# A fused three-stage decoder: new engine orders in the third stage, and a power instruction for twelve Newton operations

## The chip, the cores and the metric

One core of a Trainium2 chip runs the whole kernel. The metric is the device time of one execution in microseconds, as the median of several runs. Engines are named as the profile names them: PE (TensorE), DVE (VectorE), ACT (ScalarE), POOL (GpSimd), SP (SyncE, which here only issues transfers).

## The reference, cut to what matters

The input is 64 sequences of 64 tokens with 128 features. Three parts are added to x in turn: self attention with 16 heads of width 8, cross attention with 16 heads of width 64, and a stack of six layers of local attention and feed-forward. The change touches the third:

```python
for i in range(6):
    x = attn_layer(shift_tokens(x), Wqkv[i], q_scale[i], k_scale[i], Wo[i]) + x
    x = ffn_layer(shift_tokens(x), ln_g[i], ln_b[i], W1[i], b1[i], W2[i], b2[i]) + x

def attn_layer(x, Wqkv, qs, ksc, Wo):
    q, k, v = heads(x @ Wqkv)                    # 16 heads of 64
    q, k = l2norm(q) * qs, l2norm(k) * ksc       # t / max(norm(t), 1e-12)
    q, k = rotary(q), rotary(k)
    sim = q @ k.T * 8                            # causal, window of 32
    return (softmax(masked(sim)) @ v) @ Wo

def ffn_layer(x, g, bln, W1, b1, W2, b2):
    xn = (x - mean) / sqrt(var + 1e-5) * g + bln
    a, gate = split(xn @ W1 + b1)
    return a * gelu(gate) @ W2 + b2
```

`shift_tokens` moves the second half of the features down by one token. All arithmetic is in 32-bit floats.

## The kernel before

Two sequences make one tile of 128 tokens (partitions), so there are 32 tiles, and in the third stage 32 x 6 = 192 pairs of tile and layer, called tiles from here on. x stays in the on-chip buffers X and Y. The function `local` writes the third stage as five lists of instructions, one per engine, each a loop over i from 0 to 200. In round i an engine calls small functions, each for a tile that lies some rounds back: `query_rotary(i, 0)`, `probs_turned(i - 3, 1)`, `ff_added(i - 8)`. The work is thus a pipeline over nine tiles. The order of the calls in a round is written out by hand, and each engine works strictly in that order; semaphores count finished instructions. `Counted` turns "this half of this tile" into a count, given the order in which the halves come.

One tile goes through these steps (line numbers are those of the profile):

- SP copies Y, shifted, into `ystat` (three transfers, L1026 to L1028). PE turns it (`input_turned`), ACT copies it to `xcT`, and PE multiplies by the weights of queries (L1123), keys (L1153) and values (L1175).
- ACT squares queries (L1294) and keys (L1300). DVE rotates them: `query_rotary` (L1389) and `key_rotary` (L1403) each write two products for half of the heads, and POOL's accumulating transfers (`queries_added` L1520, `keys_added` L1526) add the two.
- The norms: query squares are summed by PE (`query_lengths`), key squares by DVE (`squares_summed`, L1424). `query_floor` (L1410) and `seeded` (L1431 to L1435) put both into `ssm`, 128 x 32, and make an integer first guess of 1/sqrt. POOL's `inverse_lengths` (L1567 to L1574) refines it with three Newton steps of four operations into `rn`.
- POOL scales keys by `rn` (`keys_scaled`, L1534), PE turns them (`keys_turned`), ACT copies them to `kT`, and PE computes `scores` (L1189, L1194). DVE takes the maximum (L1444) and subtracts it (L1450), POOL scales by the query lengths (`scores_scaled`, L1540), ACT takes exponents (L1317), DVE sums rows (L1465) and inverts (L1471), POOL normalises (`probs_scaled`, L1546).
- DVE turns the probabilities in blocks into Z (`probs_turned`, L1459); SP's `probs_moved` (L1048, L1049) moves blocks of Z between partitions with four transfers. PE multiplies by the values (`head_outputs`, L1224) and by Wo (`out_projection`, L1235), DVE adds the result to Y (`attention_added`, L1370).
- SP copies Y, shifted, into `ys` (`ff_input`, again L1026 to L1028). DVE takes `statistics` (L1417, L1419), POOL makes the deviation (`inverse_deviation`, L1552 to L1556, the middle one a power on 128 x 1), ACT applies it (`normalised`, L1327), PE turns it (`normal_turned`), ACT copies it with scale (`normal_out`, L1283). PE's `ff_in` (L1209), ACT's `gates` (L1334), DVE's `gated` (L1478), PE's `ff_out` (L1110) and DVE's `ff_added` (L1376) end the tile.

All eight PSUM banks are shared. `scores` uses bank 0, which `query_lengths` uses too, and bank 7, which first holds the keys of half 0; `ff_in` uses banks 2, 1 and 3, and bank 3 is also the one that `ff_added` reads. So `ff_in(t)` waits for `ff_added(t - 1)`, and `scores(t)` for the rotations of the next tile's keys. SP's order in a round is `layer_input(i + 1)` (`ystat`), `ff_input(i - 5)` (`ys`), then weights, if any, then `probs_moved(i - 3)`:

```python
def probs_moved(t):
    sp.wait_ge(s.p_turned.sem, s.p_turned.upto(0, t + 1))
    ...
layer_input(0)
for i in range(N + LAST + 1):
    layer_input(i + 1)
    ff_input(i - 5)
    ...
    probs_moved(i - 3)
```

Of the kernel before, what the change touches and what calls it, by code (L numbers as in the profile page):

```python
# [971 lines left out]
def local(nc, sem, m):  # L972
# [16 lines left out]
    s.x_turned, s.x_copied = sem("local_x_turned"), sem("local_x_copied")  # L989
    s.qk, s.squared, s.rotated = counted("qk", *four), counted("squared", (QUERIES, 0), (QUERIES, 1), (KEYS, 1), (KEYS, 0)), counted("rotated", *four)  # L990
    s.summed, s.seed, s.lengths = sem("local_summed"), sem("local_seed"), sem("local_lengths")
    s.q_lengths, s.q_lengths_copied = sem("local_q_lengths"), sem("local_q_lengths_copied")
# [4 lines left out]
    s.v, s.v_copied = counted("v", 1, 0), counted("v_copied", 1, 0)  # L997
    s.scores, s.mx, s.less = sem("local_scores"), counted("mx", 0, 1), counted("less", 0, 1)
    s.scaled, s.probs, s.row_sum = counted("scaled", 0, 1), counted("probs", 1, 0), counted("row_sum", 0, 1)
    s.inverse, s.normal = counted("inverse", 1, 0), counted("normal", 1, 0)  # L1000
# [89 lines left out]
    def _(pe):  # L1090
# [52 lines left out]
        def keys(t, half):  # L1143
            if exists(t):
                if half == 0:
                    pe.wait_ge(m.w_in, 64 * layer(t) + 64)
                    if t == 0:
                        pe.wait_ge(m.cross_y1, TILES)
                    at_least(pe, s.less.sem, s.less.upto(1, t - 1))
                if t < 2:  # L1150
                    at_least(pe, s.rotated.sem, s.rotated.upto((KEYS, half), t))
                cols = m.WA[:, layer(t) % 2, INNER:2 * INNER].rearrange("p (h z d) -> p z h d", z=2, d=32)
                mm(b[QK_BANK[KEYS, half]][:, :], m.xsT[:, t % 2, :], cols[:, half, :, :], start=True, stop=True)\  # L1153
                    .then_inc(s.qk.sem, 1)

        def keys_turned(t, j):
            if exists(t):
                pe.wait_ge(s.k_scaled.sem, s.k_scaled.upto(j, t + 1))
                if j == 1 and t == N - 1:
                    pe.wait_ge(s.y1, t - 3)  # L1160
                for n in range(4):
# [103 lines left out]
    def _(act):  # L1265
# [73 lines left out]
        for i in range(N + LAST + 1):  # L1339
# [15 lines left out]
            outputs_out(i - 4, 0)  # L1355
            values_out(i, 0)
            exponents(i - 2, 0)
# [5 lines left out]
    def _(dve):  # L1363
# [29 lines left out]
        def key_rotary(t, half):  # L1393

            if exists(t):
                dve.wait_ge(s.squared.sem, s.squared.upto((KEYS, half), t + 1))
                if half == 0:
                    at_least(dve, s.k_turned.sem, s.k_turned.upto(0, t))
# [27 lines left out]

        def seeded(t):
            if exists(t):
                ssm, bits = m.ssm[:, t % 2, :], m.bits[:, t % 2, :]
                dve.wait_ge(s.summed, t + 1)  # L1430
                nc.vector.tensor_scalar(ssm[:, 16:32], m.ss[:, t % 2, :], 1e-24, None, ALU.max).then_inc(s.seed, 1)  # L1431
                dve.wait_ge(s.seed, 3 * t + 1)
                nc.vector.tensor_scalar(bits, ssm.bitcast(I32), 1, None, ALU.arith_shift_right).then_inc(s.seed, 1)
                dve.wait_ge(s.seed, 3 * t + 2)
                nc.vector.tensor_scalar(m.seed[:, t % 2, :], bits, -1.0, RSQRT_MAGIC, ALU.mult, ALU.add)\  # L1435
                    .then_inc(s.seed, 1)

# [69 lines left out]
    def _(pool):  # L1507
# [15 lines left out]
        def keys_added(t):  # L1523
            if exists(t):
                pool.wait_ge(s.rotated.sem, s.rotated.upto((KEYS, 1), t + 1))
                pool.dma_start(m.RK[:, 0, :], m.RK[:, 1, :], accum_op=ALU.add).then_inc(s.k_added, 16)  # L1526

        def keys_scaled(t, j):
            if exists(t):
                if j == 1:  # L1530
                    pool.wait_ge(s.k_added, 16 * t + 16)
                    pool.wait_ge(s.lengths, 12 * t + 12)
                part = by_head(m.RK[:, 0, j * 512:(j + 1) * 512])
# [25 lines left out]
        def inverse_lengths(t):  # L1559
            if exists(t):  # L1560
                pool.wait_ge(s.seed, 3 * t + 3)
                y = m.seed[:, t % 2, :].bitcast(FP32)
                for step in range(3):
                    done = 12 * t + 4 * step
                    if step:
                        pool.wait_ge(s.lengths, done)
                    tt(m.rn_a[:, :], y, y, ALU.mult).then_inc(s.lengths, 1)  # L1567
                    pool.wait_ge(s.lengths, done + 1)
                    tt(m.rn_b[:, :], m.rn_a[:, :], m.ssm[:, t % 2, :], ALU.mult).then_inc(s.lengths, 1)
                    pool.wait_ge(s.lengths, done + 2)  # L1570
                    nc.gpsimd.tensor_scalar(m.rn_a[:, :], m.rn_b[:, :], -0.5, 1.5, ALU.mult, ALU.add)\
                        .then_inc(s.lengths, 1)
                    pool.wait_ge(s.lengths, done + 3)
                    tt(m.rn[:, t % 4, :], y, m.rn_a[:, :], ALU.mult).then_inc(s.lengths, 1)  # L1574
                    y = m.rn[:, t % 4, :]

        for i in range(N + LAST + 1):
            queries_added(i)
            probs_scaled(i - 3, 1)
            probs_scaled(i - 3, 0)  # L1580
            keys_added(i)
            inverse_deviation(i - 5)
            inverse_lengths(i)
# [54 lines left out]
```

## Time and profile before

| | us |
|---|---|
| median of 3 runs | 3696.78 (3694.6 to 3710.01) |
| profiled execution | 3706.61 |
| its span | 3704.8 |
| PE busy | 3253.5 (88%) |
| DVE busy | 2801.0 (76%) |
| POOL busy | 2652.6 (72%) |
| ACT busy | 2487.4 (67%) |

The span is that of one execution recorded by the hardware profiler, and the shares are of that span; the execution's own time lies 1.8 us over it and 9.8 us over the median of the runs. The third stage begins at about 560 us. An engine counts as busy while an instruction runs on it; issuing a transfer is not counted for SP.

### The profile page before, as it was taken

The numbers are of one execution on the slowest core, as the hardware profiler recorded it, in microseconds if no ns is written. First come the engines' busy times: TensorE is split into PE (matmuls) and PEld (weight loads), VectorE is DVE, ScalarE is ACT, GpSimd is POOL, SyncE is SP. The second block draws the span as 40 slices with busy tenths as digits, with TensorE's granted clock in tenths as the row PEclk, the third lists the DMA queues.
The fourth block names the chain that finished last, engine by engine and source line by source line (L and its number), as shares of the span: only waits on it lengthen the run. The fifth ranks groups of instructions, "written<-read, shape, count | busy, mean of one in ns | idle before, by whom it ended". The sixth has DMA issues, their size and how long they took to land.

```text
span 3704.8 us, 124977 instructions
## 1 busy us (share of the span) xinstructions
PE 3253.5 (88%) x51333; PEld 2530.0 (68%) x51333; DVE 2801.0 (76%) x5681; ACT 2487.4 (67%) x4952; POOL 2652.6 (72%) x5005
## 2 busy tenths in 40 slices
PE   8999997888888888888888888888888888888886
PEld 6778775666666666666666666766666666666665
DVE  6844446888787888887888878788778878888885
ACT  5756664676666767666667667677666766667664
POOL 5522227877787887787778877777777778777774
PEclk9999999999999999999999999999999999999999
DMA  4000004444445444444444444444444444444442
GB/s 96 3 8 8 8 6 96 102 95 94 87 103 109 92 93 90 100 104 97 94 93 89 101 104 97 90 93 95 103 103 94 95 88 98 94 98 90 97 95 52
DMA packets 280546, 310.50 MB, mean 84 GB/s; under 512 B 154281, under 2 KB 225582, under 8 KB 279982
## 3 DMA queue, kind: packets, MB, share of 16 engines
q0 software_dynamic: 58368, 201.36, 28.0%
q1 hardware_dynamic: 220892, 100.93, 10.7%
q8 instruction: 412, 6.75, 0.8%
q14 instruction: 152, 1.25, 0.1%
q10 hardware_dynamic: 722, 0.21, 0.0%
HBM read 23.63 MB, written 2.10 MB: 7 GB/s over the span
## 4 chain that ended last, share of the span: by engine, by line
PE 59%; DVE 25%; issue 8%; ACT 5%; POOL 1%; SPq 1%; DMA 1%; DVEq 0%; POOLq 0%
PE bank L1153 10%; PE bank L1235 8%; PE bank L1209 8%; PE bank L1123 8%; DVE RK L1403 6%; DVE Z L1459 6%; PE bank L1094 6%; DVE ss L1424 6%; PE bank L1110 4%; PE bank L1134 3%; ACT sq L1300 3%; ACT xnT L1283 2%; PE bank L709 2%; PE bank L722 2%; PE bank L731 2%
## 5 line engine op out<-in xcount | busy, mean ns | idle before, releaser
L1403 DVE TENSOR_TENSOR RK<-bank,tables 128x1024 f32<-128x1024 f32 x384 | 468.7, 1222 | 329.3 <-ACT sq L1300 326.2
L1209 PE MATMUL bank<-xnT,W 128*128 128x128 f32 (+1 forms) x2304 | 322.8, 294 | 350.0 <-DVE Y L1376 349.3
L1389 DVE TENSOR_TENSOR RQ<-bank,q_tables 128x1024 f32<-128x1024 f32 x384 | 452.1, 1219 | 153.3 <-ACT sq L1294 153.2
L1209 PEld LDWEIGHTS bank<-xnT,W 128*128 128x128 f32 (+1 forms) x2304 | 282.6, 190 | 371.0 <-issue 371.0
L1546 POOL TENSOR_TENSOR P<-P,inv_sum 128x512 f32<-128x512 f32 x384 | 505.7, 1634 | 5.7 <-DVE inv_sum L1471 5.7
L1534 POOL TENSOR_TENSOR RK<-RK,rn 128x512 f32<-128x512 f32 x384 | 400.2, 1042 | 28.4 <-POOL rn L1574 0.9
L1520 POOL DMA_DIRECT2D RQ<-RQ x384 | 350.1, 1041 | 97.2 <-DVE RQ L1389 90.2
L1153 PE MATMUL bank<-WA,xcT 128*128 128x512 f32 x768 | 376.8, 613 | 37.0 <-DVE P L1450 16.7
L1540 POOL TENSOR_TENSOR P<-P,rn 128x512 f32<-128x512 f32 x384 | 402.4, 1048 | 3.8 <-DVE P L1450 3.8
L1267 ACT ACTIVATE kT<-bank 128x512 f32<-128x512 f32 x384 | 229.5, 598 | 249.8 <-PE bank L1094 249.8
L1235 PE MATMUL bank<-WO,OT 128*128 128x128 f32 x3072 | 382.3, 278 | 0.0
L1175 PE MATMUL bank<-WV,xcT 128*128 128x512 f32 x768 | 380.5, 618 | 0.0
L1123 PE MATMUL bank<-xcT,WQ 128*128 128x128 f32 x3072 | 375.1, 275 | 2.4 <-ACT xcT L1267 2.2
L1235 PEld LDWEIGHTS bank<-WO,OT 128*128 128x128 f32 x3072 | 367.7, 196 | 0.0
L1123 PEld LDWEIGHTS bank<-xcT,WQ 128*128 128x128 f32 x3072 | 358.4, 192 | 4.3 <-ACT xcT L1267 4.3
L1267 ACT ACTIVATE V<-bank 128x512 f32<-128x512 f32 x384 | 231.4, 603 | 138.5 <-PE bank L1175 138.5
L1526 POOL DMA_DIRECT2D RK<-RK x192 | 168.3, 876 | 178.3 <-DVE RK L1403 168.3
L1094 PEld LDWEIGHTS bank<-ident,RK 128*128 128x128 f32 x1536 | 186.4, 141 | 111.6 <-issue 99.2
L1444 DVE TENSOR_REDUCE mx<-bank 128x8 f32<-128x512 f32 x384 | 262.0, 682 | 0.0
L1450 DVE TENSOR_TENSOR P<-bank,mx 128x512 f32<-128x512 f32 x384 | 260.6, 679 | 0.1
L1465 DVE TENSOR_REDUCE row_sum<-P 128x8 f32<-128x512 f32 x384 | 259.4, 676 | 0.0
L1459 DVE STREAM_TRANSPOSE Z<-P 128x512 f32<-128x512 f32 x384 | 248.7, 685 | 2.3 <-POOL P L1546 2.3
(166 smaller groups left out, 7567.4 us busy)
## 6 DMA issues: line engine op xcount, KB each, us to landing
RQ<-RQ POOLq DMA_DIRECT2D x384, 256.0 KB, 4.0
RK<-RK POOLq DMA_DIRECT2D x192, 512.0 KB, 4.7
Z<-Z SPq DMA_DIRECT2D x768, 64.0 KB, 2.5
WA<-in_wqkv SPq DMA_DIRECT2D x24, 256.0 KB, 2.8
ystat<-Y SPq DMA_DIRECT2D x192, 32.0 KB
ystat<-Y SPq DMA_DIRECT2D x384, 15.8 KB
ys<-Y SPq DMA_DIRECT2D x192, 32.0 KB
ys<-Y SPq DMA_DIRECT2D x384, 15.8 KB
```

What stands on the lines that cost most here:

```text
L1094: return nc.tensor.transpose(dst, src, m.ident[:, :])
L1123: last = mm(b[QK_BANK[QUERIES, j]][:, n * 128:(n + 1) * 128], m.WQ[:, layer(t) % 2, at:at + 128], m.xsT[:, t % 2, :], start=True, stop=True)
L1153: mm(b[QK_BANK[KEYS, half]][:, :], m.xsT[:, t % 2, :], cols[:, half, :, :], start=True, stop=True)\
L1209: last = mm(FF_BANK[c][0:rows, side * 128:(side + 1) * 128], m.W1[:, off + at:off + at + rows], m.xnT[:, t % 2, :], start=True, stop=True)
L1235: last = mm(OUT[:, 0:128], m.OT[:, t % 2, c * 128:c * 128 + 128], wo[:, c * 128:(c + 1) * 128], start=(c == 0), stop=(c == PAIRS - 1))
L1267: return nc.scalar.activation(dst, src, ACT.Copy)
L1389: tt(both, src.unsqueeze(1).to_broadcast([128, 2, 8, SEQ]), m.q_tables[:, layer(t), :, :].unsqueeze(2).to_broadcast([128, 2, 8, SEQ]), ALU ...
L1403: tt(both, src.unsqueeze(1).to_broadcast([128, 2, 16, 32]), tab.unsqueeze(2).to_broadcast([128, 2, 16, 32]), ALU.mult).then_inc(s.rotated. ...
L1459: nc.vector.transpose(m.Z[:, t % 2, a, 1:3, :].rearrange("p k (h n) -> p k h n", n=32), blocks)\
L1534: tt(part, part, wide(m.rn[:, t % 4, 16 + 8 * j:24 + 8 * j]), ALU.mult).then_inc(s.k_scaled.sem, 1)
L1540: tt(part, part, wide(m.rn[:, t % 4, a:16:2]), ALU.mult).then_inc(s.scaled.sem, 1)
L1546: tt(part, part, wide(m.inv_sum[:, t % 2, 8 * a:8 * a + 8]), ALU.mult).then_inc(s.normal.sem, 1)
```

## The change

On DVE `ff_added` moves from behind the transposes to right behind `statistics`, the keys are rotated half 1 first, the two transposes are parted, with the key floor and both maxima between them, and `seeded` keeps only its floor (`key_floor`). On ACT `keys_out(i - 1, 1)` moves behind the squares of keys, `normal_out` behind the second `keys_out`, and exponents, values and outputs are interleaved in another way. On POOL `queries_added` moves from the front to behind both scalings of probabilities, and `inverse_deviation` and `keys_added` come between these. `inverse_lengths` becomes one `pow` on 128 x 32. PE's order is the same, with two waits added. Cut to its core:

```diff
-    s.qk, ..., s.rotated = ..., counted("rotated", *four)
-    s.summed, s.seed, s.lengths = sem("local_summed"), sem("local_seed"), sem("local_lengths")
+    s.qk, ..., s.rotated = ..., counted("rotated", (QUERIES, 0), (QUERIES, 1), (KEYS, 1), (KEYS, 0))
+    s.summed, s.k_floor, s.lengths = sem("local_summed"), sem("local_k_floor"), sem("local_lengths")
...
         def keys(t, half):
                     at_least(pe, s.less.sem, s.less.upto(1, t - 1))
+                else:
+                    at_least(pe, s.h, 3 * (t - 7))
...
         def keys_turned(t, j):
-                if j == 1 and t == N - 1:
-                    pe.wait_ge(s.y1, t - 3)
+                if j == 1:
+                    at_least(pe, s.y1, t - 3)
...
     # ACT, one round
             squares(i, QUERIES, 1)
-            keys_out(i - 1, 1)
             squares(i, KEYS, 1)
+            keys_out(i - 1, 1)
             query_lengths_out(i)
-            normal_out(i - 6)
             squares(i, KEYS, 0)
             keys_out(i - 1, 0)
+            normal_out(i - 6)
+            exponents(i - 2, 1)
             values_out(i, 1)
-            exponents(i - 2, 1)
             outputs_out(i - 4, 1)
+            values_out(i, 0)
             outputs_out(i - 4, 0)
-            values_out(i, 0)
             exponents(i - 2, 0)
...
-        def seeded(t):
+        def key_floor(t):
             if exists(t):
                 dve.wait_ge(s.summed, t + 1)
...
         def less_maximum(t, a):
                 dve.wait_ge(s.mx.sem, s.mx.upto(a, t + 1))
+                at_least(dve, s.p_turned.sem, s.p_turned.upto(a, t - 1))
...
     # DVE, one round
             statistics(i - 5)
+            ff_added(i - 8)
+            key_rotary(i, 1)
+            query_floor(i)
             key_rotary(i, 0)
-            query_floor(i)
-            key_rotary(i, 1)
             squares_summed(i)
             probs_turned(i - 3, 1)
+            key_floor(i)
+            maximum(i - 1, 0)
+            maximum(i - 1, 1)
             probs_turned(i - 3, 0)
-            ff_added(i - 8)
-            seeded(i)
-            maximum(i - 1, 0)
-            row_sums(i - 2, 0)
+            less_maximum(i - 1, 1)
             less_maximum(i - 1, 0)
             row_sums(i - 2, 1)
-            maximum(i - 1, 1)
             attention_added(i - 4)
+            row_sums(i - 2, 0)
+            gated(i - 7)
             inverse_sums(i - 2, 1)
-            gated(i - 7)
-            less_maximum(i - 1, 1)
             inverse_sums(i - 2, 0)
...
         def keys_added(t):
-                pool.wait_ge(s.rotated.sem, s.rotated.upto((KEYS, 1), t + 1))
+                pool.wait_ge(s.rotated.sem, s.rotated.upto((KEYS, 0), t + 1))
...
         def inverse_lengths(t):
-                pool.wait_ge(s.seed, 3 * t + 3)
-                y = m.seed[:, t % 2, :].bitcast(FP32)
-                for step in range(3):
-                    done = 12 * t + 4 * step
-                    if step:
-                        pool.wait_ge(s.lengths, done)
-                    tt(m.rn_a[:, :], y, y, ALU.mult).then_inc(s.lengths, 1)
...
+                pool.wait_ge(s.k_floor, t + 1)
+                pool.wait_ge(s.q_floor, t + 1)
+                tt(m.rn[:, t % 4, :], m.ssm[:, t % 2, :], m.minus_half[:, :].to_broadcast([128, 32]), ALU.pow)\
+                    .then_inc(s.lengths, 1)
...
     # POOL, one round
-            queries_added(i)
             probs_scaled(i - 3, 1)
-            probs_scaled(i - 3, 0)
-            keys_added(i)
             inverse_deviation(i - 5)
+            keys_added(i)
+            probs_scaled(i - 3, 0)
+            queries_added(i)
             inverse_lengths(i)
```

DVE's queue in the steady part of the third stage, from the statistics to the first maxima, in the kernel before (L1376 is `ff_added`, L1459 the transposes, L1431 to L1435 `seeded`):

```order
L1417 BN_STATS stats<-ys 128x6
L1419 BN_AGGR mv<-stats 128x2
L1403 TENSOR_TENSOR RK<-bank,tables 128x2x512
L1410 TENSOR_SCALAR ssm<-bank 128x16
L1403 TENSOR_TENSOR RK<-bank,tables 128x2x512
L1424 TENSOR_REDUCE ss<-sq 128x16
L1459 STREAM_TRANSPOSE Z<-P 128x512 x2
L1376 TENSOR_TENSOR Y<-Y,bank 128x128
L1431 TENSOR_SCALAR ssm<-ss 128x16
L1433 TENSOR_SCALAR bits<-ssm 128x32
L1435 TENSOR_SCALAR seed<-bits 128x32
L1444 TENSOR_REDUCE mx<-bank 128x8
```

The same place in the changed kernel, whose lines from here on stand two or three off (L1378 is `ff_added`, L1457 the transposes):

```order
L1419 BN_STATS stats<-ys 128x6
L1421 BN_AGGR mv<-stats 128x2
L1378 TENSOR_TENSOR Y<-Y,bank 128x128
L1405 TENSOR_TENSOR RK<-bank,tables 128x2x512
L1412 TENSOR_SCALAR ssm<-bank 128x16
L1405 TENSOR_TENSOR RK<-bank,tables 128x2x512
L1426 TENSOR_REDUCE ss<-sq 128x16
L1457 STREAM_TRANSPOSE Z<-P 128x512
L1432 TENSOR_SCALAR ssm<-ss 128x16
L1441 TENSOR_REDUCE mx<-bank 128x8 x2
L1457 STREAM_TRANSPOSE Z<-P 128x512
L1448 TENSOR_TENSOR P<-bank,mx 128x512 x2
```

The feed-forward's addition now stands before the rotations, and the second transpose, for which SP's Z transfers wait, behind both maxima.

POOL's queue before, from the query transfers on (L1520 and L1526 are the accumulating transfers of queries and keys, L1546 scales probabilities, L1552 to L1556 make the deviation, L1567 to L1574 the first of three Newton steps):

```order
L1520 DMA RQ<-RQ 64x1024 x2
L1546 TENSOR_TENSOR P<-P,inv_sum 128x512 x2
L1526 DMA RK<-RK 128x1024
L1552 TENSOR_SCALAR vare<-mv 128x1
L1554 TENSOR_TENSOR rstd<-vare,minus_half 128x1
L1556 TENSOR_SCALAR nmr<-mv,rstd 128x1
L1567 TENSOR_TENSOR rn_a<-seed 128x32
L1569 TENSOR_TENSOR rn_b<-rn_a,ssm 128x32
L1571 TENSOR_SCALAR rn_a<-rn_b 128x32
L1574 TENSOR_TENSOR rn<-seed,rn_a 128x32
```

And in the changed kernel (L1544 scales probabilities, L1524 and L1518 are the transfers of keys and queries, L1561 the power, L1532 and L1538 the scalings of keys and scores):

```order
L1544 TENSOR_TENSOR P<-P,inv_sum 128x512
L1550 TENSOR_SCALAR vare<-mv 128x1
L1552 TENSOR_TENSOR rstd<-vare,minus_half 128x1
L1554 TENSOR_SCALAR nmr<-mv,rstd 128x1
L1524 DMA RK<-RK 128x1024
L1544 TENSOR_TENSOR P<-P,inv_sum 128x512
L1518 DMA RQ<-RQ 64x1024 x2
L1561 TENSOR_TENSOR rn<-ssm,minus_half 128x32
L1532 TENSOR_TENSOR RK<-RK,rn 128x512
L1538 TENSOR_TENSOR P<-P,rn 128x512
L1532 TENSOR_TENSOR RK<-RK,rn 128x512
L1538 TENSOR_TENSOR P<-P,rn 128x512
```

The query transfers now come after the keys' and the second scaling, and one instruction stands in the place of twelve.

## Rows read from the trace of the kernel before

**Rows 1.** L1417, the statistics: how often, ns min/median/max, first and last start.
```profile
L1417 DVE BATCH_NORM_STATS2 stats<-ys x192: 283/284/297, 632.8 to 3688.3; 128x6 f32<-128x128 f32 x192
```
**Rows 2.** Busy us by engine in one steady stretch; then PEclk, DMA share, GB/s.
```profile
2400.00:2800.00 400.00, 350.71 (x5401) 271.05 (x5401) 321.33 (x646) 278.39 (x549) 315.30 (x588) 0.99 0.46 97
```
**Rows 3.** Waits from 1200 to 3600 us: waiting <- releaser: us, times, longest.
```profile
PE bank L1209 <- DVE Y L1376: 273.8, 149, 2.2
...
DVE stats L1417 <- DMA ys<-Y: 32.6, 46, 3.8
```
**Rows 4.** PE's timeline, end of a tile: start, us, instruction, [idle before <-releaser].
```profile
2425.52 0.41 PE L1189 MATMUL bank<-causalb,identb 64*64 64x512 bf16 x4
2425.76 1.10 PE L1194 MATMUL bank<-kT,RQ 64*64 64x64 f32 x64
2428.70 1.57 PE L1209 MATMUL bank<-xnT,W 128*128 128x128 f32 x12 [1.83 <-DVE Y L1376]
```
**Rows 5.** SP's timeline in a quiet tile: first Z and last `ys`.
```profile
2150.06 0.69 SPq L1048 DMA_DIRECT2D Z<-Z  x1
...
2156.47 0.70 SPq L1028 DMA_DIRECT2D ys<-Y  x1
```
**Rows 6.** Transposes, last `ys` issue, statistics: first and last of 170 tiles (DVE, SP).
```profile
730.67 1.30 DVE L1459 STREAM_TRANSPOSE Z<-P 128x512 f32<-128x512 f32 x2
739.08 0.70 SPq L1028 DMA_DIRECT2D ys<-Y  x1
...
3458.64 1.29 DVE L1459 STREAM_TRANSPOSE Z<-P 128x512 f32<-128x512 f32 x2
3467.17 0.70 SPq L1028 DMA_DIRECT2D ys<-Y  x1
3469.02 0.29 DVE L1417 BATCH_NORM_STATS2 stats<-ys 128x6 f32<-128x128 f32 x1 [0.21 <-DMA ys<-Y]
```
**Rows 7.** DVE's timeline: two maxima steps, and statistics to key floor.
```profile
2413.00 0.68 DVE L1444 TENSOR_REDUCE mx<-bank 128x8 f32<-128x512 f32 x1
2413.60 0.68 DVE L1465 TENSOR_REDUCE row_sum<-P 128x8 f32<-128x512 f32 x1
...
2421.20 0.28 DVE L1417 BATCH_NORM_STATS2 stats<-ys 128x6 f32<-128x128 f32 x1
2423.60 1.22 DVE L1403 TENSOR_TENSOR RK<-bank,tables 128x1024 f32<-128x1024 f32 x1 [1.90 <-ACT sq L1300]
2424.83 1.22 DVE L1403 TENSOR_TENSOR RK<-bank,tables 128x1024 f32<-128x1024 f32 x1
2425.96 1.21 DVE L1424 TENSOR_REDUCE ss<-sq 128x16 f32<-128x1024 f32 x1
2427.08 1.29 DVE L1459 STREAM_TRANSPOSE Z<-P 128x512 f32<-128x512 f32 x2
2428.30 0.25 DVE L1376 TENSOR_TENSOR Y<-Y,bank 128x128 f32<-128x128 f32 x1
2428.47 0.16 DVE L1431 TENSOR_SCALAR ssm<-ss 128x16 f32<-128x16 f32 x1
```
**Rows 8.** Busy us by engine in 1 us while Z is issued; DMA share.
```profile
2428.00:2429.00 1.00, 0.30 (x3) 0.33 (x4) 0.93 (x6) 0.43 (x2) 0.43 (x2) 1.00 1.02 188
```
**Rows 9.** POOL's timeline: first Newton operation, keys scaled, and what it waits for.
```profile
2413.17 0.24 POOL L1567 TENSOR_TENSOR rn_a<-seed 128x32 f32<-128x32 f32 x1 [0.60 <-DVE seed L1435]
2417.09 1.04 POOL L1534 TENSOR_TENSOR RK<-RK,rn 128x512 f32<-128x512 f32 x1
2421.59 1.83 POOL L1520 DMA_DIRECT2D RQ<-RQ  x2 [0.44 <-DVE RQ L1389]
2426.34 0.87 POOL L1526 DMA_DIRECT2D RK<-RK  x1 [0.85 <-DVE RK L1403]
```
**Rows 10.** POOL's groups by form: power and addition on 128x1: busy us, mean ns.
```profile
L1554 POOL TENSOR_TENSOR rstd<-vare,minus_half 128x1 f32<-128x1 f32 x192 | 109.5, 570 | 16.0
...
L1552 POOL TENSOR_SCALAR vare<-mv 128x1 f32<-128x1 f32 x192 | 43.2, 225 | 34.7 <-DVE mv L1419 19.0
```

More of the change, by code:

```diff
@@ L989, in local @@
     s.x_turned, s.x_copied = sem("local_x_turned"), sem("local_x_copied")
-    s.qk, s.squared, s.rotated = counted("qk", *four), counted("squared", (QUERIES, 0), (QUERIES, 1), (KEYS, 1), (KEYS, 0)), counted("rotated", *four)
-    s.summed, s.seed, s.lengths = sem("local_summed"), sem("local_seed"), sem("local_lengths")
+    s.qk, s.squared, s.rotated = counted("qk", *four), counted("squared", (QUERIES, 0), (QUERIES, 1), (KEYS, 1), (KEYS, 0)), counted("rotated", (QUERIES, 0), (QUERIES, 1), (KEYS, 1), (KEYS, 0))
+    s.summed, s.k_floor, s.lengths = sem("local_summed"), sem("local_k_floor"), sem("local_lengths")
     s.q_lengths, s.q_lengths_copied = sem("local_q_lengths"), sem("local_q_lengths_copied")
@@ L997, in local @@
     s.v, s.v_copied = counted("v", 1, 0), counted("v_copied", 1, 0)
-    s.scores, s.mx, s.less = sem("local_scores"), counted("mx", 0, 1), counted("less", 0, 1)
-    s.scaled, s.probs, s.row_sum = counted("scaled", 0, 1), counted("probs", 1, 0), counted("row_sum", 0, 1)
+    s.scores, s.mx, s.less = sem("local_scores"), counted("mx", 0, 1), counted("less", 1, 0)
+    s.scaled, s.probs, s.row_sum = counted("scaled", 0, 1), counted("probs", 1, 0), counted("row_sum", 1, 0)
     s.inverse, s.normal = counted("inverse", 1, 0), counted("normal", 1, 0)
@@ L1396, in key_rotary @@
                 dve.wait_ge(s.squared.sem, s.squared.upto((KEYS, half), t + 1))
-                if half == 0:
+                if half == 1:
                     at_least(dve, s.k_turned.sem, s.k_turned.upto(0, t))
@@ L1425, in squares_summed @@
                                         ALU.add).then_inc(s.summed, 1)
-        def seeded(t):
+        def key_floor(t):
             if exists(t):
-                ssm, bits = m.ssm[:, t % 2, :], m.bits[:, t % 2, :]
                 dve.wait_ge(s.summed, t + 1)
[L1431 to L1436, printed above, removed]
+                nc.vector.tensor_scalar(m.ssm[:, t % 2, 16:32], m.ss[:, t % 2, :], 1e-24, None, ALU.max)\
+                    .then_inc(s.k_floor, 1)
         def by_head(ap):
@@ L1531, in keys_scaled @@
                     pool.wait_ge(s.k_added, 16 * t + 16)
-                    pool.wait_ge(s.lengths, 12 * t + 12)
+                    pool.wait_ge(s.lengths, t + 1)
                 part = by_head(m.RK[:, 0, j * 512:(j + 1) * 512])
@@ L1560, in inverse_lengths @@
             if exists(t):
-                pool.wait_ge(s.seed, 3 * t + 3)
-                y = m.seed[:, t % 2, :].bitcast(FP32)
-                for step in range(3):
-                    done = 12 * t + 4 * step
-                    if step:
-                        pool.wait_ge(s.lengths, done)
-                    tt(m.rn_a[:, :], y, y, ALU.mult).then_inc(s.lengths, 1)
[L1568 to L1575, printed above, removed]
+                pool.wait_ge(s.k_floor, t + 1)
+                pool.wait_ge(s.q_floor, t + 1)
+                tt(m.rn[:, t % 4, :], m.ssm[:, t % 2, :], m.minus_half[:, :].to_broadcast([128, 32]), ALU.pow)\
+                    .then_inc(s.lengths, 1)
         for i in range(N + LAST + 1):
+            probs_scaled(i - 3, 1)
+            inverse_deviation(i - 5)
+            keys_added(i)
+            probs_scaled(i - 3, 0)
             queries_added(i)
-            probs_scaled(i - 3, 1)
-            probs_scaled(i - 3, 0)
-            keys_added(i)
-            inverse_deviation(i - 5)
             inverse_lengths(i)
```

## The prediction

> **What bounds the kernel now.** I read the stage first, then the waits, then one tile on each engine. The third stage handles 192 tiles; the statistics instruction that each tile has once starts at 632.8 us for the first and at 3688.3 us for the last [rows 1], so one tile takes (3688.3 - 632.8) / 191 = 16.00 us. Times 191, that is nearly the whole kernel, and every number below is one of microseconds per tile. In a steady stretch of 400 us, 25 tiles, PE is busy 350.7 us, 14.0 per tile, DVE 12.9, POOL 12.6, ACT 11.1, with the clock at 0.99 of the 2.4 GHz level [rows 2]. PE is the fullest engine and yet idles: its one large wait stands before the feed-forward matmuls, 1.83 to 1.84 us per tile, released by DVE's addition at L1376 [rows 3, 4]. In a tile's timeline the scores end at 2426.86 and the feed-forward starts at 2428.70 [rows 4]; everything else on PE is back to back, so PE alone would need 16.00 - 1.83 = 14.17 per tile.
>
> Beside that stands a second circle, which the waits show only faintly: DVE waited 32.6 us for the `ys` transfers in this stretch, 46 times [rows 3]. It runs like this. When the second transpose into Z is done (L1459), SP issues four Z transfers, then three for `ystat`, then three for `ys`, strictly in that order. DVE's statistics at L1417 wait for the three `ys` to land, and the next tile's transposes stand behind the statistics on DVE. So every tile goes once through DVE and once through SP's queue. In a quiet tile SP starts the first Z at 2150.06 and the last `ys` at 2156.47 [rows 5], 6.4 us after the end of the transpose. Over the 170 tiles between 731 and 3470 us I find 6.92 us on average; the first has 739.08 - 731.97 = 7.11, the last 3467.17 - 3459.93 = 7.24 [rows 6]. From the last issue to the start of the waiting statistics are 3469.02 - 3467.17 = 1.85 us [rows 6] (the median of all that waited is 1.89). SP's half is 6.92 + 1.89 = 8.81. DVE's half, statistics at 2421.20 to the end of the transposes at 2428.37, is 7.17 [rows 7]. Together 15.98 of a period of 16.00: this circle is almost as tight as PE's.
>
> **The change part by part.**
> *DVE's addition `ff_added` moves up,* from behind both transposes to right behind the statistics. PE's feed-forward then no longer waits for it: worth up to 1.83, if nothing else is late. What is late next is the question of this prediction.
> *Two integer operations go from DVE* (0.18 each): 12.9 - 0.4 = 12.5 of DVE's work per tile. It isn't the bound, so nothing by itself.
> *DVE's half of the circle.* Before, DVE stood idle for 1.90 in it, waiting for ACT's squares of the keys [rows 7]. ACT's new order makes the second square ahead of `normal_out` and of one copy, and the rotations are taken in the order in which squares come, so I take this wait as gone. But new work comes in between: `ff_added`, the key floor, both maxima. From the starts in [rows 7]: statistics to next 0.50, addition 0.17, first rotation and query floor 2424.83 - 2423.60 = 1.23, second 1.13, sums 1.12, first transpose 0.61, key floor 0.19, two maxima 2 x 0.60, last transpose 0.68 to its end. Sum 6.83, against 7.17. The 1.90 of idle time is nearly all filled up again by work. The maxima need scores, and PE may begin these only after the second key rotation, now: 0.50 + 0.17 + 1.23 + 1.22 = 3.12 into DVE's half, plus 0.1 and PE's 1.34 (2425.52 to 2426.86, [rows 4]), is 4.6, while DVE comes to them at 4.95. No wait, by 0.35.
> *SP's half* keeps its ten issues and its order. 8.81. So the circle asks for 6.83 + 8.81 = 15.64, above PE's 14.17: it becomes the bound, with PE now waiting some 1.5 us for the key rotation before its scores.
> *One more effect on SP.* When Z was issued, the DMA engines were full (share 1.02) with the accumulating transfer of keys [rows 8]. The new POOL order issues that transfer and the two for queries closer together, ending later against Z. A full tile shows that issues in such a stretch can take longer, since 6.41 becomes 6.92 on average. I add 0.1 of the same kind as a choice, the bounds being -0.5 (every tile quiet) and +0.5 (a second time the excess seen). That gives 15.7.
> *POOL's queue.* `queries_added` with its two transfers goes behind `keys_added` and one scaling, and the deviation goes ahead of `keys_added`, so that the scaling of the second half and both query transfers now queue behind the wait for the last key rotation. The query transfers are needed only by the scores a tile later; the second scaling ends 3.2 + 0.9 + 1.1 = 5.2 into the DVE half and its transpose starts at 6.1. Hidden, by 0.9. The two waits added on PE (for `h` at the second keys matmul, `y1` at the turned keys) find their work done 0.8 and more before; priced at nothing, and PE has 1.5 to give.
> *Newton becomes one power.* The twelve operations took 2417.09 - 2413.17 = 3.92 [rows 9]. All else on POOL: 15.98, less the waits of 0.60, 0.44 and 0.85 [rows 9], less 3.92, is 10.2. So POOL has room for a power instruction of 15.7 - 10.2 = 5.5 us before it sets the pace, and the shortening itself is worth nothing. No power on 128x32 is in the trace. The nearest row is the power on 128x1: 570 ns, beside 225 ns for a plain addition of that size [rows 10]. The lower end is 0.6, if the extra 345 ns are spent once; the upper end 0.23 + 32 x 0.345 = 11.3, if they are spent per column. The one row that bears on it has a single column and can't choose. I take a value below 5.5, as a guess: a single column pays the whole latency of the operation, 32 may overlap; below 150 ns per column the price doesn't matter.
> On this the Trainium skill, GPSIMD Engine Reference, sections 1 and 2, says that each of the eight cores serves 16 partitions with vectors of 16 floats. By that rule a column is one vector per core and 32 columns are 32 evaluations, which speaks for the upper end; no run here shows which, and the sum by it would be that of the second rival below.
>
> *Sum.* 191 x (16.00 - 15.70) = 57 us. The profiled execution took 3706.6, which becomes 3649; it lay 9.8 above the median of the runs (3696.8), so the forecast for the median is 3640 us.
>
> **The rivals.**
> *Only PE counts.* If the circle through SP had slack that I don't see, the tile would take 14.17 and the kernel 3697 - 191 x 1.83 = 3347. For it speaks that PE's wait is the largest in the list; against it that the two halves of the circle already add up to the period. 0.06.
> *Power by the column.* POOL would set the pace at 10.2 + p: even with before at p = 5.8 us (175 ns per column), and at the upper end of 11.3 a tile takes 21.5 and the kernel 3697 + 191 x 5.5 = 4750. For it: the 345 ns of a single column, the only power price in the trace. Against: at less than half of that per column it doesn't happen. The place is L1561 of the changed kernel, and the keys' scaling behind it. 0.19. This is the rival on the slow side.
> *The circle gives nothing back.* If Z's and `ystat`'s issues are stretched by 0.3 more than I took, the tile takes 16.0: 3697, no change, 0.17. If by 0.5 and more, 16.2 or worse: from 3735 on, 0.09.
>
> **How the numbers follow.** About 0.5%, 18 us or 0.1 us per tile, is what a measurement of this kernel can tell from no change. My forecast case (15.1 to 15.9 per tile) has 0.49. Faster: 0.49 + 0.06 = 0.55. Same: 0.17. Slower: 0.19 + 0.09 = 0.28. The range: at its low end every tile is quiet, 6.41 + 1.85 + 6.83 = 15.09, so 3697 - 191 x 0.9 = 3525; at its high end 16.25, or 3745. It leaves out the PE-only case and most of the costly power, some 0.2. The forecast's own range is 3525 to 3678.
>
> **What would show it.** PE's wait before L1209 should be gone, and one of some 1.5 us stand before the scores (L1189), released by DVE's key rotation. DVE's wait for `ys` should come in nearly all tiles, for 2 us or so, and the chain of waits should run through DVE and `DMA ys`. DVE's half should read 6.8 and SP's 8.8 to 9.0. The power should read under 5.5 us; POOL should show waits. The forecast is wrong if PE is full without a wait (then SP's half was shorter than 7.3), or if POOL has no idle time left.

## The result, and the profile after

The changed kernel takes 3876.55 us (median of 4 runs, 3868.85 to 3883.13) against 3699.64 for the kernel before (four runs, where the forecast had three): 1.047 times as long, with a 95% interval of 1.044 to 1.051. The forecast was 3640, in a range from 3525 to 3745. The profiled execution has a span of 3873.3 us.

The statistics of the third stage once per tile (how often, ns min/median/max, first and last start), as in [rows 1]:

```profile
L1419 DVE BATCH_NORM_STATS2 stats<-ys x192: 293/294/297, 646.7 to 3854.7; 128x6 f32<-128x128 f32 x192
```

A tile takes (3854.7 - 646.7) / 191 = 16.80 us, in place of 16.00. That is 153 of the 177 us; some 14 more lie ahead of the first statistics, the rest behind the last and in the difference between executions. The 16.80 counts the short tiles at the end of the pipeline too; between 729 and 3472 us a tile takes 16.93 on average, where it took 16.14 before.

Busy time in the stretch of [rows 2] (PE, PEld, DVE, ACT, POOL; PEclk, DMA share, GB/s), then the page's chain that ended last, by engine:

```profile
2400.00:2800.00 400.00, 351.74 (x5187) 265.40 (x5188) 309.73 (x565) 267.48 (x521) 362.60 (x312) 0.96 0.43 90
PE 23%; DVE 22%; POOL 21%; SPq 19%; issue 8%; DMA 5%; ACT 0%; POOLq 0%; DVEq 0%
```

No engine stands out: the chain goes through PE, DVE, POOL and SP's queue in nearly equal parts. PE's granted clock is 0.96 where it was 0.99. The waits between 1200 and 3600 us answer to [rows 3]:

```profile
DVE stats L1419 <- DMA ys<-Y: 470.1, 142, 4.4
...
PE bank L1094 <- POOL RK L1532: 273.7, 141, 2.2
POOL RK L1524 <- DVE RK L1405: 157.6, 137, 2.1
...
PE bank L1191 <- DVE RK L1405: 22.8, 40, 1.4
```

PE's wait for the feed-forward's addition is no longer in the list. In its place DVE waits for `ys` in every recorded tile, 3.3 us each, and PE waits 1.9 us for keys that POOL has scaled. One tile on DVE, with the same columns as [rows 7]:

```profile
2420.43 0.30 DVE L1419 BATCH_NORM_STATS2 stats<-ys 128x6 f32<-128x128 f32 x1 [2.73 <-DMA ys<-Y]
2420.76 0.18 DVE L1421 BATCH_NORM_AGGREGATE mv<-stats 128x2 f32<-128x6 f32 x1
2420.86 0.25 DVE L1378 TENSOR_TENSOR Y<-Y,bank 128x128 f32<-128x128 f32 x1
2421.03 1.22 DVE L1405 TENSOR_TENSOR RK<-bank,tables 128x1024 f32<-128x1024 f32 x1
...
2424.50 0.70 DVE L1457 STREAM_TRANSPOSE Z<-P 128x512 f32<-128x512 f32 x1
2425.12 0.71 DVE L1432 TENSOR_SCALAR ssm<-ss 128x16 f32<-128x16 f32 x1
2425.75 1.28 DVE L1441 TENSOR_REDUCE mx<-bank 128x8 f32<-128x512 f32 x2
2426.95 0.70 DVE L1457 STREAM_TRANSPOSE Z<-P 128x512 f32<-128x512 f32 x1
```

From the statistics to the end of the second transpose are 2427.65 - 2420.43 = 7.22 us; the forecast said 6.83. All steps are within 0.07 of the forecast but one: the key floor (L1432) takes 0.71 us where it took 0.16 [rows 7], and 0.63 from start to start where the sum had 0.19. It ends at 2425.83, 0.04 after POOL's scaling of probabilities (2424.44 and 1.35 us long, below). SP's queue behind that tile:

```profile
2427.67 0.69 SPq L1048 DMA_DIRECT2D Z<-Z  x1
2428.41 1.34 SPq L1049 DMA_DIRECT2D Z<-Z  x1
...
2434.75 0.70 SPq L1028 DMA_DIRECT2D ys<-Y  x1
```

The second Z issue takes 1.34 us, twice the 0.67 of a quiet tile. Over 163 tiles from 729 to 3472 us SP's half from the transpose to the last `ys` issue is 7.47 us on average; it was 6.92 [rows 6]. The landing, 1.88, is as before. The circle is 7.22 + 7.47 + 1.88 = 16.57, in which 7.22 and 1.88 are medians: the usual tile. DVE's half is 7.57 on average, and 7.57 + 7.47 + 1.89 = 16.93. Most of the 0.35 between 7.22 and 7.57 is what DVE waits for PE in some tiles, as shown below. And POOL:

```profile
2423.76 0.95 POOL L1524 DMA_DIRECT2D RK<-RK  x1 [0.48 <-DVE RK L1405]
2424.44 1.35 POOL L1544 TENSOR_TENSOR P<-P,inv_sum 128x512 f32<-128x512 f32 x1
2425.43 2.05 POOL L1518 DMA_DIRECT2D RQ<-RQ  x2
2426.60 6.37 POOL L1561 TENSOR_TENSOR rn<-ssm,minus_half 128x32 f32<-128x32 f32 x1
2433.11 1.04 POOL L1532 TENSOR_TENSOR RK<-RK,rn 128x512 f32<-128x512 f32 x1
```

The power reads 6.37 us, but 0.88 of it lies over the end of the query transfers' issue (2425.43 + 2.05 = 2427.48); from there to the next start are 5.6. So POOL too is nearly full: 0.48 us of wait in this tile of 16.2, and 1.1 on average (157.6 us of waits for the rotation in 142 tiles, above). In the next tile PE's record changes. First the feed-forward's output matmuls in two successive tiles, then the stretch from 2434 to 2438 us with its PEclk of 0.58 (columns as in [rows 2]):

```profile
2419.13 0.94 PE L1110 MATMUL bank<-W,H 128*128 128x128 f32 x6
...
2435.88 1.65 PE L1110 MATMUL bank<-W,H 128*128 128x128 f32 x6
```

```profile
2434.00:2438.00 4.00, 3.79 (x30) 3.14 (x31) 0.77 (x3) 1.36 (x3) 4.00 (x5) 0.58 0.09 19
```

PE had stood idle for 2.06 us before its keys, and then worked at the 1.2 GHz level for over 3 us, so the same matmuls took 1.65 in place of 0.94. The addition and the key rotations on DVE, which wait for them, came late, and that tile was 1.1 us longer than the one before (POOL's power starts at 2426.60 and 2443.98, after 2410.36 and 2426.60). The 161 tiles from 729 to 3472 us fall into two groups in this way. In 67 the granted clock was down at some time between 3 us before the statistics and 1 us behind them, and these took 17.37 us on average, with 8.03 in DVE's half; the other 94 took 16.62, with 7.24. PE began to turn the keys 2.82 us before the statistics in both groups, so the keys were not late. The lower clock thus adds 0.31 us to the mean tile. This compares tiles of one run; no run changes the clock alone.

### The profile page after: what moved, and what is told of

It reads as the page before. It is cut to its first block, busy times and chain, and to the rows that moved or that the text cites. A ratio compares the mean times of both kernels' runs of the same rounds, so it can differ in the third digit from the quotient of the medians.

```text
span 3873.3 us, 123240 instructions
## 1 busy us (share of the span) xinstructions
PE 3385.1 (87%) x51333; PEld 2573.5 (66%) x51333; DVE 2836.3 (73%) x5297; ACT 2508.2 (65%) x4952; POOL 3149.1 (81%) x2893
## 4 chain that ended last, share of the span: by engine, by line
PE 23%; DVE 22%; POOL 21%; SPq 19%; issue 8%; DMA 5%; ACT 0%; POOLq 0%; DVEq 0%
POOL rn L1561 12%; DVE RK L1405 9%; SPq L1049 6%; DMA ys<-Y 5%; POOL RQ L1518 5%; SPq L1027 4%; SPq L1048 4%; PE bank L1094 3%; DVE Z L1457 3%; SPq L1026 3%; PE bank L1110 3%; DVE ss L1426 3%; POOL RK L1532 2%; SPq L1028 2%; POOL RK L1524 2%
## 5 line engine op out<-in xcount | busy, mean ns | idle before, releaser
L1561 POOL TENSOR_TENSOR rn<-ssm,minus_half 128x32 f32<-128x32 f32 x192 | 1222.1, 6365 | 0.0
L1094 PE MATMUL bank<-ident,RK 128*128 128x128 f32 x1536 | 286.8, 317 | 389.0 <-POOL RK L1532 389.0
L1094 PEld LDWEIGHTS bank<-ident,RK 128*128 128x128 f32 x1536 | 196.2, 160 | 560.9 <-POOL RK L1532 549.2
L1419 DVE BATCH_NORM_STATS2 stats<-ys 128x6 f32<-128x128 f32 x192 | 56.6, 295 | 633.1 <-DMA ys<-Y 633.1
L1405 DVE TENSOR_TENSOR RK<-bank,tables 128x1024 f32<-128x1024 f32 x384 | 467.1, 1218 | 46.3 <-PE bank L1094 45.4
L1544 POOL TENSOR_TENSOR P<-P,inv_sum 128x512 f32<-128x512 f32 x384 | 458.9, 1195 | 3.4 <-DVE inv_sum L1469 3.4
L1532 POOL TENSOR_TENSOR RK<-RK,rn 128x512 f32<-128x512 f32 x384 | 399.3, 1040 | 27.8 <-POOL rn L1561 0.4
L1538 POOL TENSOR_TENSOR P<-P,rn 128x512 f32<-128x512 f32 x384 | 400.5, 1043 | 2.6 <-DVE P L1448 2.6
L1518 POOL DMA_DIRECT2D RQ<-RQ x384 | 393.7, 1315 | 0.0
L1524 POOL DMA_DIRECT2D RK<-RK x192 | 181.9, 948 | 240.5 <-DVE RK L1405 226.3
L1211 PE MATMUL bank<-xnT,W 128*128 128x128 f32 (+1 forms) x2304 | 310.2, 285 | 7.6 <-DVE Y L1378 7.6
L1302 ACT ACTIVATE sq<-bank 128x512 f32<-128x512 f32 x384 | 228.3, 595 | 101.8 <-PE bank L1155 101.7
L1211 PEld LDWEIGHTS bank<-xnT,W 128*128 128x128 f32 (+1 forms) x2304 | 267.0, 181 | 21.2 <-issue 8.7
```

Of the source, the lines that this page charges most:

```text
L1094: return nc.tensor.transpose(dst, src, m.ident[:, :])
L1211: last = mm(FF_BANK[c][0:rows, side * 128:(side + 1) * 128], m.W1[:, off + at:off + at + rows], m.xnT[:, t % 2, :], start=True, stop=True)
L1405: tt(both, src.unsqueeze(1).to_broadcast([128, 2, 16, 32]), tab.unsqueeze(2).to_broadcast([128, 2, 16, 32]), ALU.mult).then_inc(s.rotated. ...
L1518: pool.dma_start(m.RQ[z:128:2, t % 2, 0, :], m.RQ[1 - z:128:2, t % 2, 1, :], accum_op=ALU.add)\
L1532: tt(part, part, wide(m.rn[:, t % 4, 16 + 8 * j:24 + 8 * j]), ALU.mult).then_inc(s.k_scaled.sem, 1)
L1538: tt(part, part, wide(m.rn[:, t % 4, a:16:2]), ALU.mult).then_inc(s.scaled.sem, 1)
```

## The experiments

Two causes were to be told apart: the circle through SP, and the power, which fills POOL. Each run is compared with the kernel before on the same chip; tile times come from the first and last statistics, as above. Runs with a constant leave out the inverse lengths.

### The power alone

The kernel before, with `key_floor` for `seeded` and the one `pow` for Newton:

```diff
+                tt(m.rn[:, t % 4, :], m.ssm[:, t % 2, :], m.minus_half[:, :].to_broadcast([128, 32]), ALU.pow)\
+                    .then_inc(s.lengths, 1)
```

> The old orders, with the key floor in the place of the seed and the one power in the place of the twelve Newton operations. Theory (two circles: POOL's own queue at 10.2 us plus the power, and the circle through SP): the power takes 6.37 us here too, so POOL needs 16.6 us a tile or more, against 16.0 before: 3815 us or more, and POOL shows next to no idle time. Rival (the power is hidden, and only the new orders lengthened the SP circle): 3700 us.

Measured: 3704.16 us, ratio 1.001 (0.9995 to 1.002). My theory fell here and its rival held. On POOL's timeline:

```profile
2413.70 0.26 POOL L1551 TENSOR_SCALAR nmr<-mv,rstd 128x1 f32<-128x1 f32 x1
2414.13 5.43 POOL L1558 TENSOR_TENSOR rn<-ssm,minus_half 128x32 f32<-128x32 f32 x1 [0.16 <-DVE ssm L1430]
2419.70 1.04 POOL L1529 TENSOR_TENSOR RK<-RK,rn 128x512 f32<-128x512 f32 x1
...
2427.73 0.87 POOL L1521 DMA_DIRECT2D RK<-RK  x1 [0.18 <-issue]
```

The power behind a plain instruction takes 5.43 us, not 6.37, and POOL's tile comes to 15.6 with waits of 0.2 and 0.2: it just fits into 16.0. POOL's slack is nearly used up, but no one waits longer for it.

### The orders alone

The changed kernel with `seeded` and Newton put back:

```diff
-            key_floor(i)
+            seeded(i)
```

> The new orders with the seed and the twelve Newton operations back. Theory: POOL then needs 10.2 + 3.9 = 14.1 us a tile and no longer sets the pace, but the circle through SP does: DVE's half 7.2 + SP's half 7.5 + 1.9 for the landing = 16.6, perhaps 0.3 less where the key floor no longer waits: 16.3 to 16.6, or 3755 to 3815 us. Rival (the power alone made it slower): 15.6 a tile as forecast, 3640 us or less.

Measured: 3868.58 us, ratio 1.045 (1.042 to 1.047); the tile takes 16.78. Somewhat over the expected range, and far from the rival's 3640. The new orders are nearly as slow without the power as with it. In part this is chance: the two operations that come back with the seed lie in DVE's half, which is 7.66 in the median in place of 7.22. The next run is without them.

### A constant in the place of the power

```diff
-                tt(m.rn[:, t % 4, :], m.ssm[:, t % 2, :], m.minus_half[:, :].to_broadcast([128, 32]), ALU.pow)\
+                nc.gpsimd.tensor_scalar(m.rn[:, t % 4, :], m.ssm[:, t % 2, :], 0.0, 0.1, ALU.mult, ALU.add)\
                     .then_inc(s.lengths, 1)
```

> The new orders, and in the place of the power an operation that writes the constant 0.1 (some 0.22 us), so that POOL has 10.4 us a tile: the inverse lengths are left out. Theory: the SP circle alone, as in the run with the new orders and Newton, 16.3 to 16.6 a tile, 3755 to 3815 us. Rival (the power alone): 14.2 to 15.6, 3350 to 3640 us.

Measured: 3826.99 us, ratio 1.034 (1.031 to 1.037); 16.64 a tile. Waits between 1200 and 3600 us:

```profile
POOL vare L1550 <- DVE mv L1421: 526.0, 143, 6.1
...
DVE stats L1419 <- DMA ys<-Y: 453.1, 143, 5.6
```

POOL now waits 3.7 us per tile for the statistics, and these for `ys`. With a POOL that is idle for over a third of the time the tile is still 16.64: DVE's half 7.23, SP's 7.41, the landing 1.88, in sum 16.52 for the usual tile, and in averages 7.33 + 7.41 + 2.05 = 16.79, which is the mean tile of that stretch. The SP circle alone holds the new orders there. PE's large wait now stands where the forecast had put it, before the scores:

```profile
PE bank L1191 <- DVE RK L1405: 319.3, 141, 4.7
```

### `ys` ahead of `ystat`

```diff
-            layer_input(i + 1)
             ff_input(i - 5)
+            layer_input(i + 1)
```

> The changed kernel with ff_input ahead of layer_input on SP, so that the three ystat issues (2.2 us) leave the circle. Theory: the SP circle falls to 14.4, but POOL with the power still needs 16.6: 16.6 to 16.8, 3815 to 3870 us, with DVE's wait for ys gone or small. Rival (the SP circle alone is the bound): 15.0 or less, under 3500 us.

Measured: 3768.06 us, ratio 1.017 (1.014 to 1.020); 16.22 a tile. Lower than expected, but still slower than before. Three issues are out of the SP circle, and another one shows. PE's and DVE's timelines in one tile:

```profile
2434.57 0.66 PE L1094 MATMUL bank<-ident,RK 128*128 128x128 f32 x4 [1.88 <-POOL RK L1532]
```

```profile
2436.70 0.29 DVE L1378 TENSOR_TENSOR Y<-Y,bank 128x128 f32<-128x128 f32 x1 [1.35 <-PE bank L1110]
2437.34 1.23 DVE L1405 TENSOR_TENSOR RK<-bank,tables 128x1024 f32<-128x1024 f32 x1 [0.35 <-PE bank L1094]
```

PE waits for the keys that POOL scales behind the power; DVE's addition and first rotation wait for PE; POOL's transfer of keys waits for the rotation. From one such transfer to the next are 2440.08 - 2424.12 = 15.96 us. Of 167 such periods, the 117 in which the clock stayed near full take 16.0 on average; the other 50 (mean clock under 0.97) take 17.1. That is a second circle, of the same length as the old tile while the clock is full and longer than the SP circle of 16.57 when it is not, made of the power, the queue on POOL around it and the new order on DVE.

### Both at once

The constant and `ys` first together, then Newton and `ys` first together.

> Both suspects taken away at once from the changed kernel: the constant in the place of the power (the inverse lengths are left out) and ys ahead of ystat on SP. Theory (two circles, each enough alone to hold the tile at 16.2 to 16.7): the SP circle is then 7.2 + 5.3 + 1.9 = 14.4 and POOL has room, so a tile takes 14.4 to 14.8: 3395 to 3470 us. Rival (a third thing, such as the waits on PE or the lower clock after them, holds the new orders back): 15.5 or more, 3600 us and up.

Measured: 3394.93 us, ratio 0.918 (0.915 to 0.920), at the low end of what was expected.

> The new orders, the twelve Newton operations back, and ys ahead of ystat on SP. Theory: SP circle 7.7 (the seed's two operations lie in DVE's half) + 5.3 + 1.9 = 14.9, POOL's chain by way of PE and DVE 16.0 - 5.6 + 3.9 = 14.3: 14.9 to 15.2 a tile, 3490 to 3545 us, faster than before. Rival (Newton's chain on POOL costs as much here as the power): 16.2, 3740 us.

Measured: 3448.21 us, ratio 0.932 (0.930 to 0.934), 14.65 a tile; the theory had 14.9 to 15.2. The constant alone moved the changed kernel by 50 us, the order on SP alone by 108, and both together by 482. That is how two circles of nearly one length behave: each hides what the other is worth. No third cause is needed for the slowdown, and the lower clock goes with the two circles: between 1200 and 3200 us it is 1.00 in both runs.

### The query transfers early

The run with the constant, and `queries_added(i)` back at the front of POOL's round.

> The run with the constant (inverse lengths left out), and queries_added back at the front of POOL's round, so that its two transfers are over before Z is issued. Theory (the query transfers stretch SP's Z issues from 0.70 to 1.1 us and more): SP's half falls from 7.4 to 6.9 and the tile from 16.6 to 16.1: 3730 us. Rival (the longer issues come from something else, such as the keys' transfer): 3827 us as in the run with the constant.

Measured: 3883.96 us, ratio 1.048 (1.046 to 1.051); 16.94 a tile, slower by 57 us than the run with the constant where 97 less were expected. The first half of the theory held: SP's half fell to 6.7 us on average, its second Z issue to 0.67 in the median, from 1.36. But:

```profile
2417.28 0.70 SPq L1028 DMA_DIRECT2D ys<-Y  x1
```

```profile
2420.47 0.29 DVE L1419 BATCH_NORM_STATS2 stats<-ys 128x6 f32<-128x128 f32 x1 [3.78 <-DMA ys<-Y]
```

```profile
2416.99 1.75 POOL L1518 DMA_DIRECT2D RQ<-RQ  x2 [1.23 <-DVE RQ L1391]
```

The query transfers now start 0.3 us before the last `ys`, and this lands after 3.2 us in place of 1.9 (the median of 161 tiles is 3.08). Late, they stretch the issues of Z; early, the landing of `ys`. Both ends are on the circle.

### The key floor late

The run with the constant, and `key_floor` behind the second transpose.

> The run with the constant (inverse lengths left out), and the key floor behind the second transpose. Theory: the 0.7 us that the floor now takes, most of it a wait for POOL's scaling, leaves DVE's half of the circle: 16.6 - 0.65 = 16.0 a tile, 3700 us; if the wait is tied to POOL, the operation should read near 0.16 us at the new place, where POOL issues transfers or the constant. Rival (what comes behind the floor would have waited as long): 3827 us.

Measured: 3773.14 us, ratio 1.020 (1.018 to 1.021); 16.39 a tile, 54 us less where 127 were expected. DVE's timeline:

```profile
2427.96 0.29 DVE L1419 BATCH_NORM_STATS2 stats<-ys 128x6 f32<-128x128 f32 x1 [3.77 <-DMA ys<-Y]
...
2432.66 1.25 DVE L1441 TENSOR_REDUCE mx<-bank 128x8 f32<-128x512 f32 x2
2433.83 0.69 DVE L1457 STREAM_TRANSPOSE Z<-P 128x512 f32<-128x512 f32 x1
2434.44 0.14 DVE L1432 TENSOR_SCALAR ssm<-ss 128x16 f32<-128x16 f32 x1
```

At its new place the floor takes 0.13 to 0.14 us in nearly all tiles: the 0.55 more were a wait for POOL's scaling. DVE's half is 6.56 here, 0.66 less. The rival, that the transpose behind would wait as long, did not hold: only 8 of 384 transposes waited for POOL, 5.3 us in all. But most of the gain is taken back at two other places. The maxima come earlier and now wait for PE's scores in some tiles, 0.20 us a tile on average, and SP's half grows from 7.41 to 7.62:

```profile
2435.29 1.14 SPq L1049 DMA_DIRECT2D Z<-Z  x1
2436.46 1.25 SPq L1048 DMA_DIRECT2D Z<-Z  x1
```

Z's issues start 0.66 us earlier against POOL's query transfers, and the third is stretched too (0.62 to 1.13 on average, while the second falls from 1.53 to 1.19). The theory held for the floor and failed in taking the rest of the circle as fixed.

### The old orders, with one and with two moves

> The kernel before with ys ahead of ystat on SP, and nothing else. Theory: in the old orders PE's wait for the feed-forward's addition sets the tile at 16.0 and the SP circle was only just as long, so shortening it gives little: the small waits for ys go, 3680 to 3697 us. Rival (the SP circle was the true bound of the old orders too): 3500 us or less.

Measured: 3698.89 us, ratio 0.998 (0.997 to 1.000). The old orders were bound by PE's wait.

For the second run `ff_added(i - 8)` goes right behind `statistics(i - 5)`, with the changed kernel's two waits on PE, and one more in `ff_in`, since nothing else orders it behind the key rotation that reads its bank:

```diff
+                pe.wait_ge(s.rotated.sem, s.rotated.upto((KEYS, 1), min(t + 8, N)))
```

> The kernel before with two moves only: the feed-forward's addition right behind the statistics on DVE (with the waits on PE that this needs), and ys ahead of ystat on SP. Theory: PE's wait goes and the SP circle has room (5.4 + 4.7 + 1.9 = 12.0), and the next bound is POOL's chain from the last key rotation over the seed, Newton, the four scalings, the query transfers and the probabilities: 3.0 + 3.9 + 4.1 + 3.9 = 14.9 a tile, 3490 to 3530 us. Rival (the rest of the new orders is needed for the gain): 3690 us.

Measured: 3593.59 us, ratio 0.970 (0.968 to 0.972). Faster, but 60 us short of the theory. POOL's waits for the rotation (1.1 us) and the seed (0.4) remain, so its chain of instructions isn't the whole circle. The chain that ended last is DVE for 46% and PE for 38% in this run, with nothing from SP, which speaks for a circle through these two; it was not followed further.

### A version faster than both

From the run with Newton and `ys` first. On DVE the seed goes ahead of both transposes and the maxima behind; on POOL both scalings stand together:

```diff
             squares_summed(i)
+            seeded(i)
             probs_turned(i - 3, 1)
-            seeded(i)
+            probs_turned(i - 3, 0)
             maximum(i - 1, 0)
             maximum(i - 1, 1)
-            probs_turned(i - 3, 0)
...
             probs_scaled(i - 3, 1)
+            probs_scaled(i - 3, 0)
             inverse_deviation(i - 5)
             keys_added(i)
-            probs_scaled(i - 3, 0)
```

> The run with new orders, Newton and ys first, and besides: on DVE the seed ahead of both transposes and the maxima behind them, on POOL both scalings of probabilities ahead of the deviation and the keys' transfer. Theory: DVE's half falls from 7.7 to 6.0 and the SP circle to 12.8, so PE (14.2) and POOL (14.0) remain: 14.2 to 14.5 a tile, 3350 to 3410 us. Rival (the clock of PE or POOL's chain already bounds the run before it): 3448 us as there.

Measured: 3340.91 us, ratio 0.903 (0.900 to 0.905), 9 us under the expected range. Busy time from 1200 to 3200 us (columns as in [rows 2]), and the statistics:

```profile
1200.00:3200.00 2000.00, 1973.45 (x30611) 1508.52 (x30610) 1845.33 (x3689) 1575.24 (x3109) 1789.88 (x3389) 1.00 0.53 109
```

```profile
L1419 DVE BATCH_NORM_STATS2 stats<-ys x192: 293/294/297, 627.7 to 3314.7; 128x6 f32<-128x128 f32 x192
```

PE is busy for 98.7% of the time, at full clock; a tile takes 14.07 us, under the 14.17 that PE was held to need.

### The price of the power

> The changed kernel with the power on the 16 columns of the keys only and the constant 0.1 on those of the queries (their inverse lengths are left out). Theory (the price goes by the column, 0.41 us and 0.157 per column from 0.57 at one column and 5.43 at 32): the power reads 2.9 us, or up to 0.9 more where it stands behind the query transfers in the record; the tile stays at the SP circle, 16.6: 3820 to 3830 us. Rival (the price is by the instruction): 5.4 us.

Measured: 3845.71 us, ratio 1.038 (1.036 to 1.041), 16 us over the expected 3820 to 3830 for the tile at the SP circle (median of two runs).

```profile
L1562 POOL TENSOR_TENSOR rn<-ssm,minus_half x192: 2917/2922/2931, 578.6 to 3780.3; 128x16 f32<-128x16 f32 x192
```

With 0.57 us at one column [rows 10], 2.92 at 16 and 5.43 at 32, the power costs 157 ns per column above some 0.4 us. The price goes by the column.

## Why the prediction was wrong

**Right: what the move of `ff_added` does, and what is late next.** PE's wait for it went, and the circle through DVE and SP's queue became a bound, with DVE waiting for `ys` in every tile. The runs show both: 3448 with that circle shortened, 3869 with it whole (Newton in both). The 15.98 that the forecast gave this circle in the kernel before is somewhat too long, since it took DVE's 7.17 from one tile; over 170 tiles that half is 6.98 on average, and `ys` first alone gave 5 us there.

**Wrong: the length of that circle, and so the sign.** The forecast had 6.83 + 8.81 + 0.1 = 15.7; measured were 7.22 + 7.47 + 1.88 = 16.57 for the usual tile. Two terms were too small, and both on the same ground, a duration carried over to a place where other work runs beside it. A third, DVE waiting for PE within its half, was put at nothing.
- *The key floor, 0.19 in the sum, took 0.63 start to start.* Before, POOL stood idle at that point, waiting for the seed. In the new order it scales probabilities then.
- *SP's issues.* "I add 0.1 of the same kind as a choice, the bounds being -0.5 and +0.5": it was +0.55. The step had named the cause, POOL's transfers running into Z's issues, and the run with early query transfers bears it out. The value was taken near the middle with no row behind it.
- *DVE's waits for PE.* They make up most of the 0.35 by which DVE's mean half, 7.57, lies over the 7.22 of the usual tile, and come from the second circle and the clock, below.

By its time the result falls to the forecast's third rival, at its larger size, which had 0.09; by its mechanism only in part. The issues were stretched by 0.45 more than taken, which by itself gives 16.15; the rest of the slowdown is the floor and the waits for PE, which no rival had.

**Right by luck: the power under 5.5 us.** It takes 5.43, and alone it is free in the old orders. But the price goes by the column, at 157 ns where 150 was given as the limit. It stayed below 5.5 because a column costs 157 ns and not the 345 of the upper end; whether columns overlap is not shown. The Trainium skill, GPSIMD Engine Reference, sections 1 and 2, says that each core serves 16 partitions with vectors of 16 floats, so that a column is one vector per core. The trace agrees in that the price grows in line with the columns: 0.57, 2.92 and 5.43 us for 1, 16 and 32.

**Wrong: that the power doesn't matter below 5.5.** The forecast compared POOL's own sum with the tile. The second circle wasn't seen: power, scaled keys, PE, the addition and the key rotation on DVE, and back to POOL, 15.96 even with `ys` first and the clock full. It exists only because the new order puts the rotation behind the addition, which waits for PE. With the SP circle at 16.57 it was nearly as long, and PE's wait stood before the turned keys, not before the scores as forecast. With the constant in the place of the power it stands before the scores.

**Not forecast: PE's clock.** It was 0.96 in place of 0.99. The tiles with the lower clock took 17.37 us and the others 16.62, which is 0.31 in the mean tile, of some 0.8 by which it grew. In the run with the constant the mean clock was as low (0.961), but DVE waited for PE only 0.03 us a tile in its half of the circle: there all 40 slow stretches between 1200 and 3200 us follow a wait that stands before the scores, while in the changed kernel all 49 follow the wait before the keys.

**Right: what PE alone would allow.** The sum gave 3347 if only PE counted, and the last version reaches 3341. The room was there; in the changed kernel the two circles kept it closed.

## What to carry to other kernels

Before an order is changed by hand, add up every circle that passes through more than one queue, the transfer queue's issues and the landing included; a circle that already fills nearly the whole period will take most of the gain, and a wait list shows it only as a few small waits. Moving work out of such a circle also shifts it against the other queues, so part of the gain can be lost again in its other half. When two circles are of one length, each single experiment says that neither matters much: take both away in one run. And an instruction's duration holds for its neighbourhood; one that runs beside another engine's work for the first time needs a range of its own.

## What the runs showed of the hardware

A DVE operation on 128x16 takes 0.13 to 0.16 us alone and 0.71 where POOL is scaling a 128x512 tile; in each of the 189 tiles of the changed kernel in which the two meet it ended 0.04 us after POOL did, and at another place it was short again. The addition of X and Y (128x128, both in the on-chip buffers) took 0.29 us each of 32 times before and up to 1.01 in the changed kernel, where POOL's scalings run beside it. The Trainium skill, SBUF — State Buffer, "SBUF: two separate sides", says that VectorE and GpSimd share one pair of ports as an exclusive lock held for a whole instruction, for some forms of VectorE operation; this trace agrees for the key floor, while the large DVE operations beside POOL kept their durations (L1405: 1.218 us on average, 1.222 before).

Issuing a transfer from SP takes 0.59 to 0.69 us for Z when it is undisturbed and up to 2.2 in the changed kernel, where POOL's accumulating transfers are in flight. A small transfer (`ys`) lands after 1.9 us in the median there and after 3.1 where POOL's query transfers start just ahead of it.

PE's granted clock fell to the 1.2 GHz level after a wait of 2.06 us and stayed at 1.00 after one of 1.86 in the tile before. Its mean over the span was 0.945 with early query transfers, where PE waited for up to 5.6 us, and 0.993 in the last version, where no wait of PE between 1200 and 3200 us was over 1 us.
